# Weighting the last chunk on VectorE, a room of its own for the z half of the gate weights, and a new order of the last steps of a token mixer

## What is computed

```python
logits = gelu(gate_in @ gW1 + gb1) @ gW2 + gb2
probs = softmax(logits / tau) * (1 - sum(eps)) + eps
o = einsum('blhp,blhpd->blhd', probs, paths)          # 5 paths, 4 heads of 64
o = o * rsqrt(mean(o * o, -1) + 1e-5) * norm_w
z = x + o.reshape(b, L, D) @ Wo
# the recurrence: z_t is the input of step t
gate = sigmoid(h @ Wh.T + z_t @ Wz.T + b)
h = tanh(h * (1 - alpha) + gate * z_t)
out = z + experts(h)                                  # top-1 of 8
```

## Time and profile before

| | us |
|---|---|
| median of 3 runs | 989.67 (988.26 to 993.84) |
| the profiled execution, its own time | 992.66 |
| its span in the trace | 990.8 |
| TensorE busy, share of the span | 731.5, 74% |
| VectorE | 657.4, 66% |
| ScalarE | 514.0, 52% |
| GpSimd | 257.7, 26% |
| mean granted TensorE clock | 0.862 of full |

### The profile page before, as it was taken

The page is one execution under the profiler, slowest core; times in us unless marked ns, Lnnn a source line. Parts: engine busy times, 40 slices in busy tenths (PEclk is TensorE's granted clock), DMA queues, the critical chain, the costliest instruction groups (busy, mean ns, idle before and its releaser), DMA issues. The chain is left out here.

```text
span 990.8 us, 15103 instructions
## 1 busy us (share of the span) xinstructions
PE 731.5 (74%) x5694; PEld 454.9 (46%) x5694; DVE 657.4 (66%) x929; ACT 514.0 (52%) x842; POOL 257.7 (26%) x231
## 2 busy tenths in 40 slices
PE   3840009787776296783986878999997599999995
PEld 1310004334556285772533443444446467777763
DVE  5999976967745987367698845999997133333331
ACT  5878764763333253554552348999993122222221
POOL 0000000001102000000333403998983224333331
PEclk9975558998889669997987889999995599999997
DMA  5720000002890000002000027400003801111100
GB/s 201 258 91 0 0 0 22 1 0 71 230 241 13 1 4 24 3 3 99 1 0 1 22 74 276 168 0 1 0 1 97 309 25 41 45 46 35 35 12 0
DMA packets 35881, 60.68 MB, mean 61 GB/s; under 512 B 8187, under 2 KB 22523, under 8 KB 35426
## 3 DMA queue, kind: packets, MB, share of 16 engines
q1 hardware_dynamic: 30194, 51.31, 16.4%
q0 software_dynamic: 3312, 6.31, 2.1%
q10 hardware_dynamic: 2304, 2.10, 0.6%
HBM read 55.23 MB, written 7.21 MB: 63 GB/s over the span
## 5 line engine op out<-in xcount | busy, mean ns | idle before, releaser
L1964 ACT ACTIVATE xT<-x_tr,moe_b 128x128 f32<-128x128 f32 x184 | 50.1, 384 | 151.6 <-PE x_tr L1929 151.6
L1911 PE MATMUL x_hid<-w,moe_xt 128*128 x184 | 86.0, 612 | 1.4 <-DVE moe_xt L2055 1.1
L1920 PE MATMUL x_y<-w,xT 128*128 x368 | 85.0, 385 | 2.1 <-ACT xT L1964 2.1
L1159 POOL TENSOR_TENSOR path<-path,mix_pr 128x1280 f32<-128x1280 f32 x16 | 38.7, 2448 | 146.3 <-DVE mix_pr L1393 146.3
L2062 DVE COPY xT<-x_hid 128x512 f32<-128x512 f32 x46 | 31.8, 692 | 64.8 <-PE x_hid L1911 64.8
L1920 PEld LDWEIGHTS x_y<-w,xT 128*128 128x128 f32 x368 | 69.4, 193 | 11.6 <-issue 2.8
L1711 DVE TENSOR_TENSOR_SCAN w<-r_bank,w 128x512 f32<-128x512 f32 x56 | 69.7, 1246 | 0.2 <-ACT r_bank L1645 0.2
L217 PE MATMUL bad_sum<-spike_bad,ones 128*128 128x16 f32 x2 | 0.6, 386 | 85.2 <-ACT spike_outside L183 85.2
L1585 PE MATMUL r_bank<-recur_h_other,w1h 128*128 128x512 f32 x128 | 60.3, 593 | 0.7 <-ACT recur_h_other L1625 0.7
L1581 PE MATMUL r_bank<-hs,eye 128*128 128x512 f32 x112 | 57.2, 592 | 1.8 <-DVE h L1692 1.8
L213 PE MATMUL w_bank<-spike_wbuf,spike_pick 128*128 128x512 f32 x80 | 39.0, 645 | 22.7 <-DMA spike_wbuf<-in_gW 22.7
(11 more groups left out here) (286 smaller groups left out, 1812.4 us busy)
## 6 DMA issues: line engine op xcount, KB each, us to landing
spike_wbuf<-in_gW SPq DMA_DIRECT2D x8, 1280.0 KB, 6.3
w<-in_w1T SPq DMA_DIRECT2D x8, 1024.0 KB, 12.2
w<-in_w2T SPq DMA_DIRECT2D x8, 1024.0 KB, 15.2
fir_band<-in_band_l SPq DMA_DIRECT2D x11, 512.0 KB
fir_band<-in_band_m SPq DMA_DIRECT2D x11, 312.0 KB
mix_st<-in_band_l SPq DMA_DIRECT2D x5, 512.0 KB
xT<-in_xT SPq DMA_DIRECT2D x4, 512.0 KB, 6.5
xT<-in_xT SPq DMA_DIRECT2D x2, 1024.0 KB, 6.1
```

What stands on the lines that cost most here:

```text
L1159: nc.gpsimd.tensor_tensor(x, x, w, ALU.mult).then_inc(s.weighted, 1)
L1911: last = nc.tensor.matmul(hid_bank[n][:], xt[:, c, :], m.w1[:, bass.ds(e, 1), c, n * N:(n + 1) * N].rearrange("p o n -> p (o n)"), start=( ...
L1920: last = nc.tensor.matmul(y_bank[:], ht[:, k, :], w2[:, bass.ds(e, 1), k, :].rearrange("p o n -> p (o n)"), start=(k == 0), stop=(k == K2 ...
L1964: nc.scalar.activation(ht[:, k, :], tr_bank[k // (K2 // 2)][:, k % (K2 // 2) * P:(k % (K2 // 2) + 1) * P], ACT.Relu, bias=b1[:, bass.ds(e, ...
```

## The change

It does six things. The last four of the 16 multiplications go from GpSimd to VectorE (`weigh`). The z half of the gate weights gets a tile of its own, `wz`, loaded when `mix` begins; only the h half is still loaded late into the old room. gate_part(0) goes ahead of project(2) on TensorE, and the other gate parts, rows and projections change places. ScalarE's copies follow that order. A sigmoid of one column (`warm`) is put behind the last square root of `mix`. In `recur`, four of the eight guesses are made ahead of the first sigmoid, and the other four one behind each of the first four sigmoids; TensorE's first identity product no longer waits for the constants.

```diff
@@ mix: sync
+            sp.dma_start(wz[:], d.wgT[D:].rearrange("(k p) n -> p k n", p=P)).then_inc(s.wg_in, 16)
             sp.wait_ge(s.hid_psum, 4 * CHUNKS)
-            sp.dma_start(m.wg, d.wgT.rearrange("(k p) n -> p k n", p=P)).then_inc(s.wg_in, 16)
+            sp.dma_start(m.wg, d.wgT[0:D].rearrange("(k p) n -> p k n", p=P)).then_inc(s.wh_in, 16)
...
@@ mix: gpsimd
-            for a in range(CHUNKS * TILES):
-                n, k = divmod(a, TILES)
-                x = path(a).rearrange("q p (h v) -> q p h v", v=DV)
-                w = pr[n % 2][:, k].rearrange("q h p -> q p h").unsqueeze(3).broadcast_to([P, NP, H, DV])
-                pool.wait_ge(s.probs_ready, n + 1)
-                nc.gpsimd.tensor_tensor(x, x, w, ALU.mult).then_inc(s.weighted, 1)
+            for a in range(LAST * TILES):
+                pool.wait_ge(s.probs_ready, a // TILES + 1)
+                nc.gpsimd.tensor_tensor(by_head(a), by_head(a), weights(a), ALU.mult).then_inc(s.weighted, 1)
@@ mix: scalar
                 expo(i)
+            zw_out(0)
             turned_back(2)
-            zw_out(0)
             rows_out(0)
             root(3)
             zw_out(1)
+            turned_back(3)
             rows_out(1)
             root(4)
-            turned_back(3)
+            nc.scalar.activation(warm[:], m.bias_g[:, 0:1], ACT.Sigmoid)
+            turned_back(4)
+            rows_out(2)
             zw_out(2)
-            rows_out(2)
-            turned_back(4)
             rows_out(3)
             zw_out(3)
@@ mix: tensor, gate_part
-                        last = nc.tensor.matmul(hid_bank[c][:], m.wg[:, C + k, c * P:(c + 1) * P],
+                        last = nc.tensor.matmul(hid_bank[c][:], wz[:, k, c * P:(c + 1) * P],
@@ mix: tensor
+            gate_part(0)
             project(2)
-            gate_part(0)
             rows(0)
             gate_part(1)
+            project(3)
             rows(1)
-            project(3)
+            project(4)
+            rows(2)
             gate_part(2)
-            rows(2)
-            project(4)
             rows(3)
             gate_part(3)
@@ mix: vector
+            def weigh(a):
+                nc.vector.tensor_tensor(by_head(a), by_head(a), weights(a), ALU.mult).then_inc(s.last_weighted, 1)
...
+            dve.wait_ge(s.probs_ready, CHUNKS)
+            weigh(12)
+            weigh(13)
             combine(12)
             combine(13)
             residual(2)
             squares(3)
+            weigh(14)
+            normed(3)
+            weigh(15)
             combine(14)
             combine(15)
-            normed(3)
             squares(4)
             normed(4)
@@ recur: tensor
-            pe.wait_ge(s.leaks, 5)
...
                 nc.tensor.matmul(out, m.eye[:], zw[:, c * B + b, t0:t0 + N], start=True, stop=False)
+                if u == 0:
+                    pe.wait_ge(s.leaks, 5)
@@ recur: scalar   (GUESSED = UNITS // 2)
-            for u in range(UNITS):
+            def guess(u):
...
+            for u in range(GUESSED):
+                guess(u)
...
             for u in range(ALL + LAG_F):
                 if u < ALL:
                     sigmoid(u)
+                if u + GUESSED < UNITS:
+                    guess(u + GUESSED)
                 if u >= LAG_F:
                     value(u - LAG_F)
                     slope(u - LAG_F)
```

More of the change, by code:

```diff
@@ L1099, in mix @@
         wo = sb("wo", [P, C, D])
+        wz = sb("wz", [P, C, D])
         nw = sb("nw", [P, 1])
@@ L1110, in mix @@
         o_t = sb("o_t", [P, C, N])
+        warm = sb("warm", [P, 1])
         bank = lambda n: own.enter_context(nc.psum_tensor(n, [P, N], F32))
@@ L1119, in mix @@
                  "ms_ready", "root_ready", "rs_ready", "on_ready", "ot_psum", "ot_ready", "wo_psum", "z_ready",
-                 "wg_in", "zw_psum", "zw_ready", "row_psum", "row_ready", "rows_out")
+                 "wg_in", "wh_in", "zw_psum", "zw_ready", "row_psum", "row_ready", "rows_out", "last_weighted")
         s = namedtuple("MixSemaphores", names)(*(sem("m_" + n) for n in names))
@@ L1123, in mix @@
         path = lambda a: m.path[:, a]
+        by_head = lambda a: path(a).rearrange("q p (h v) -> q p h v", v=DV)
+        weights = lambda a: (pr[a // TILES % 2][:, a % TILES].rearrange("q h p -> q p h").unsqueeze(3)
+                             .broadcast_to([P, NP, H, DV]))
         where = lambda n: (n // (T // N), (n % (T // N)) * N)
@@ L1149, in _ @@
             sp.wait_ge(s.x_in, 16 * C)
+            sp.wait_ge(s.wh_in, 16)
             sp.wait_ge(s.rows_out, 16 * 2 * CHUNKS)
@@ L1397, in combine @@
                 x = path(a)
-                dve.wait_ge(s.weighted, a + 1)
+                if n < LAST:
+                    dve.wait_ge(s.weighted, a + 1)
+                else:
+                    dve.wait_ge(s.last_weighted, k + 1)
                 nc.vector.tensor_tensor(x[:, 0:2], x[:, 0:2], x[:, 2:4], ALU.add).then_inc(s.adding, 1)
@@ L1533, in recur @@
         LAG_F, LAG_R, LAG_SCAN, LAG_ADD = 1, 1, 2, 3
+        GUESSED = UNITS // 2
         def unit(u):
@@ L2136, in layer_kernel @@
         m.w1h = sb("w1h", [P, C, HF])
-        m.wg = m.w1h[:].rearrange("p c n -> p (c n)").rearrange("p (k n) -> p k n", n=D)
+        m.wg = m.w1h[:].rearrange("p c n -> p (c n)")[:, 0:C * D].rearrange("p (k n) -> p k n", n=D)
         m.bias_g = sb("bias_g", [P, C])
```

## The result

The changed kernel takes 989.97 us (median of 20 runs, 984.41 to 995.46), the kernel before 994.02 (median of 20, 987.98 to 999.93). The ratio is 0.9958, 95% interval 0.9940 to 0.9976: some 4.2 us less, 2.4 to 6.0. Three executions that were clearly slower than the rest (1882, 1213 and 1005 us) are left out of all ratios. The measured 989.97 lies inside the predicted range (983.5 to 991.0) and 2.4 us above the predicted 987.6. The base was too low and the gain too small, and the two errors took part of each other away: that the number came so near is in part luck.

A forecast was written before the change was run, and what follows sets the result against it. It took TensorE, never idle, to bound the recurrence, and no engine to be full at the end of mix. A mix gain of 2.2 us less a recurrence loss of 0.15 gave -2.05, from 989.67 to 987.6; range 983.5 to 991.0.

The forecast's parts named there:

- The base: Whole kernel: 989.67 us, median of three runs spread by 5.6, from which the predicted gain was subtracted.
- the lower clock behind the hole: End of mix, TensorE: project(4)'s product takes 3.57 us instead of 1.99, the gate part behind 4.07 instead of 3.43.
- The first rival: End of mix: the clock stays up in the last hole, gain 4.8 us, giving 985.0; chance 0.22.
- VectorE saves 6 us early and gives them back: End of mix: two multiplications, the wait for root(3) and the order use up the saving; part 4's norm comes no earlier.
- The hole of 3.3 us: End of mix: TensorE waits 575.9 to 579.2 ahead of project(4); the earlier 3.28 us wait served as nearest row.
- Loss 0.15: Recurrence: it ends about 0.15 us later, argument 55 being 0.35 later and a 0.2 us tail wait gone.
- VectorE has no slack to follow: Recurrence: VectorE needs 2.539 us a unit against TensorE's 2.577, so its later start uses up TensorE's 1.3 us lead.
- TensorE pacing the recurrence: Rival, recurrence: VectorE starts early enough, so TensorE's 1.3 us stay, giving 986.2; chance 0.12.
- VectorE not catching up at all: Rival, recurrence: at 2.577 us a unit, argument 55 comes 2.2 later, less 0.2, giving 989.5; chance 0.07.
- The warming: Start of recurrence: the early sigmoid saves two 1.28 us table loads; rival that both return, 988.9, chance 0.08.
- The drain of 1.38 us: ScalarE's table switch, end of mix: by the skill page, some 1.38 us behind the load, 0.8 us less gain; not assumed.
- The dear multiplication: Rival, end of mix: VectorE's multiplications take 2.87 us each, the end comes 2.9 later, giving 990.5; chance 0.07.

The follow-up runs named there:

- e1: Changed kernel with the recurrence as before: eight guesses ahead of the first sigmoid, TensorE waiting for constants, no warming sigmoid; ratio to the kernel before 0.9963.
- e2: Changed kernel with all eight guesses ahead of the first sigmoid, table still warmed; ratio to the kernel before 0.9960.
- e5: Changed kernel with all 16 multiplications on GpSimd again, other steps in the changed order; ratio to the kernel before 1.0018.
- e6: Changed kernel with gate_part(0) behind project(2) again, on TensorE and in ScalarE's copies; ratio to the kernel before 1.0000.
- e9: Kernel of e6 with root(3) ahead of zw_out(0) and rows_out(0), root(4) ahead of rows_out(1) on ScalarE; ratio to the kernel before 0.9966.
- e10: Kernel of e5 with root(4) ahead of rows_out(1) on ScalarE; ratio to the kernel before 0.9999.
- e3: Changed kernel with gate_part(2) ahead of project(4) on TensorE and zw_out(2) ahead of turned_back(4) on ScalarE; 985.43 us, ratio to the kernel before 0.9909.
- e8: The kernel before, unchanged, traced a second time; mix 40.28 us, last scan at 152.06, experts 232.47; no ratio given.
- e11: Kernel before with only the last four multiplications moved to VectorE, in the changed kernel's places; ratio to the kernel before 1.0042.
- e7: e4 with root(3) ahead of rows_out(0), weigh(14) ahead of squares(3), residual(2) behind it, warming sigmoid behind the last projection copies; 982.46 us, ratio to kernel before 0.9891.
- e4: Changed kernel with the edits of e2 and e3 together; 985.26 us, ratio to the kernel before 0.9899.

## Why the prediction was right, and where it was not

**The steps of `mix`, from the end of the logits.** (The end of a step of TensorE is here, as in the prediction, the start of its next instruction.) End of gate_part(0): predicted 5.14, measured 5.05. Product of project(2): 7.44, 7.43. root(3): 12.49, 12.56. Norm of part 3: 16.1, 16.2. Product of project(3): 17.3, 17.4. root(4): 20.7, 20.8. Norm of part 4: 23.4, 23.5. The multiplication of 1.48 us, taken from a reduction of the same length, was right.

**The term that was mis-sized** is the last one, the lower clock behind the hole. I took the row of before whole: transposes, product and gate part all slowed, 2.6 us in all (593.8 against the 591.2 at full clock). Measured: the transposes at full clock, the product of project(4) at 24.7 instead of 25.1, over at 28.1 instead of 28.6, and gate_part(2) at full clock. That makes 1.17 us, so 3.36 instead of 2.2. It is the same in the traces of e1 and e2 (36.93, 36.97). The first rival (clock up throughout, 4.8) was off on the other side.

**"VectorE saves 6 us early and gives them back"** was right in the sum and wrong in what it said of the cause. I saw root(3) wait for rows_out(0), and priced it; and the sum starts root(4) when ScalarE is free of the copies of rows(1) (576.45, VectorE done at 576.2). But among the causes that I named, ScalarE's copies ahead of root(4) are missing, and the theories of e5 and e6 took the last norm for VectorE's own pace. By e5, e6, e9 and e10 it is ScalarE's queue: root(4) behind rows_out(1). In the changed kernel the two are 0.2 us apart, and so the sum came out under either reading: that is luck. The hole of 3.3 us, taken as the nearest row for the clock because of its equal length, had another cause in the kernel before.

**The recurrence.** State product predicted at 1.2, measured 1.30; residual 12.8, 12.93; argument(3) 15.1, 15.27; argument(55) 147.15, 147.14. Loss 0.15, measured 0.02. "VectorE has no slack to follow" is shown for the changed kernel by its rate of 2.536 to the end, by e2 (the residual early, and the 1.25 us are there) and by the accident in e3. That the gain of TensorE and the loss of VectorE cancel to 0.02 us is a matter of their sizes, 1.2 and 1.12.

**The rivals.** TensorE pacing the recurrence fell with e1 for the changed kernel, though its condition (VectorE starts early enough) was a sound one: e2 meets it, and the 1.25 us stay; VectorE not catching up at all fell by its rate, 2.536. The warming does what it says over the barrier: no load at 593.41. The drain of 1.38 us that comes on top of a load by the Trainium skill, page "ScalarE: Activation LUTs", section "What ACT_TABLE_LOAD costs", doesn't show here either: the load starts at 577.84, right behind the square root (over at 577.82), the warming sigmoid starts 1.30 us behind it, and the copies follow at once. The dear multiplication fell: 1.48 us each, not 2.87.

**What was left over.** 3.36 us of `mix` and nothing of the recurrence make 3.4, inside the measured 2.4 to 6.0. The 3.45 us of the experts in the two traces are the clock's (e8), not a gain. The base was the median of three runs.

## What to carry to other kernels

A hole that stays the same length, to the hundredth, while the work ahead of it is moved (3.27 us in the changed kernel, e5 and e6) points to a tie and not to a lack of speed: some engine's queue ties its end to its own beginning, here TensorE's rows by way of ScalarE's copies to the square root. Look in each in-order queue for the step on the path that stands behind one that isn't, and move that, before any work is moved from one engine to another. The equal length alone is no proof (that of the kernel before, 3.28, had another cause); one exchange in the queue, as in e9 and e10, is. The multiplications alone won nothing here (e11), and with the order around them they were worth 2 us (e10) to 6 us (e5) by the traces.

Where two engines run at nearly the same rate (2.54 and 2.58 us a unit), which of them sets the end depends on when each starts. In the changed kernel it is VectorE: TensorE's earlier start is worth nothing, and a delay of VectorE by 1.7 us at argument(3) is still 1.7 us at the last scan (e3). In the kernel before, e2 and e11 it is TensorE, and its 1.7 us of delay in e11 reach the end though VectorE's argument(3) is only 0.66 us late. So an earlier start pays only as far as the other engine's allows: find both before one is moved.

## What the hardware showed that was not expected

- TensorE's clock behind 32 tiny products (20 columns each) was at its lower level for part of the next stage in the changed kernel, e1, e2, e5, e7 and e10 (5.38 us for eight passes) and stayed up in e3 and e4 (3.68), from the same instructions, with the edits of e3 and e4 behind them. e7 has the order of e3 and e4 there, and 5.38. It is 1.7 us of luck in a trace, as large as most edits here; stage times of one trace each are to be compared with that in mind.
- At the start of the recurrence a wait of TensorE 0.7 us longer (e3), or none longer at all (e11), went with a fall of the clock in the first unit (3.65 us for 1.88); in e7, with a wait 0.64 longer, and in the kernel before the clock stayed up (1.96 and 1.98). What decides it stays open.
- The experts, whose code no edit touches, took 3.45 us more in one trace than in another from the same work, by a later rise of the clock and a second fall in the last product (5.40 us for 3.72). It was met in five of the thirteen traces.
- The rows' last transfers landed early in e4 and late in e3 and e7, with the same order of steps in e3 and e4: TensorE's idle time ahead of the recurrence was 1.20 us in e4 and 1.94 in e3.
